# An eight-core transformer layer on Trainium2: V's second half, Wo's load, up's weights, the late AV copies and the x1 transposes at other places

## The reference, cut to what matters

```python
# x: (8, 2048, 1024) f32; 16 heads of 64
q, k, v = x @ Wq.T + bq, x @ Wk.T + bk, x @ Wv.T + bv
scores = einsum('bqhd,bkhd->bhqk', q, k) * hd ** -0.5
scores = scores * exp(-alpha * abs(i - j))        # i, j: positions
att = softmax(scores) @ v                         # per head, then joined
x1 = layernorm(x + att @ Wo.T + bo)
gate, up = fp4_linear(x1, w_gate), fp4_linear(x1, w_up)     # 2816 wide
h = silu(gate) * up
out = layernorm(x1 + fp4_linear(h, w_down))
# fp4_linear quantises both operands in blocks of 16 along the contracted
# dimension to an E2M1 grid and multiplies the dequantised values
```

## Time and profile before

| | us |
|---|---|
| median of 3 runs | 1275.07 |
| lowest, highest | 1273.63, 1281.92 |
| the profiled execution: its time | 1273.74 |
| its span on the slowest core (core 2) | 1272.2 |
| spans of all cores | 1261.7 to 1272.2 |

### The profile page before, as it was taken

The page is one execution under the profiler, slowest core; times in us unless marked ns, Lnnn a source line. Parts: engine busy times, 40 slices in busy tenths (PEclk is TensorE's granted clock), DMA queues, the critical chain, the costliest instruction groups (busy, mean ns, idle before and its releaser), DMA issues.

```text
span 1272.2 us, 18941 instructions; the slowest of 8 cores (1261.7 to 1272.2 us)
## 1 busy us (share of the span) xinstructions
PE 1156.1 (91%) x5787; PEld 460.6 (36%) x5856; DVE 1032.2 (81%) x1328; ACT 706.2 (56%) x841; POOL 257.7 (20%) x444
## 2 busy tenths in 40 slices
PE   3969999999999889999988886999999999999994
PEld 1413333333333223332322232444444444444442
DVE  4659999998988999997995476689888888888873
ACT  2148989888889899998998122222222222222221
POOL 1002222222222222322322343000101111111001
PEclk9979999999999999998998898999999999999998
DMA  9455646465454556675559369933333333334231
GB/s 247 166 116 137 146 118 156 117 127 126 110 140 120 140 129 152 148 167 151 159 157 261 86 205 299 315 113 110 81 91 82 81 93 81 81 92 126 67 68 61
DMA packets 180118, 172.58 MB, mean 136 GB/s; under 512 B 141938, under 2 KB 141938, under 8 KB 178484
## 3 DMA queue, kind: packets, MB, share of 16 engines
q1 hardware_dynamic: 165716, 138.72, 40.0%
q0 software_dynamic: 14304, 32.65, 10.9%
HBM read 111.30 MB, written 34.34 MB: 114 GB/s over the span
## 4 chain that ended last, share of the span: by engine, by line
PE 49%; DVE 16%; DMA 11%; issue 10%; ACT 9%; SPq 2%; POOL 2%; DVEq 0%; POOLq 0%; ACTq 0%
PE ps L1072 15%; PE ps L622 10%; PE ps L1154 8%; PE ps L501 7%; PE ps L456 6%; ACT PT L593 5%; PE ps L451 3%; DMA ring<-x_scr 3%; DVE fr L240 2%; DMA wos<-wo 2%; DMA vst<-wv 2%; DVE attnT L671 1%; ACT PT L601 1%; DVE qr L240 1%; SPq L1025 1%
## 5 line engine op out<-in xcount | busy, mean ns | idle before, releaser
L593 ACT ACTIVATE PT<-ps,tab 128x1024 bf16<-128x1024 f32 x384 | 414.1, 1130 | 72.5 <-PE ps L501 72.0
L622 PE MATMUL ps<-PT,V 128*128 128x512 bf16 (+1 forms) x1234 | 290.9, 341 | 10.1 <-issue 3.9
L501 PE MATMUL ps<-Q,KT 64*128 64x512 bf16 (+1 forms) x1280 | 205.8, 343 | 28.1 <-DVE SD L552 12.8
L1072 PE MATMUL ps<-wgT,x1qT 128*128 128x512 bf16 (+1 forms) x768 | 169.4, 364 | 10.8 <-DMA x1qT<-x1q 9.3
L1072 PE MATMUL ps<-wuT,x1qT 128*128 128x512 bf16 (+1 forms) x768 | 168.2, 362 | 0.5 <-DVE fs L242 0.3
L456 PE MATMUL ps<-xTs,wqk 128*128 128x512 bf16 x499 | 140.2, 386 | 26.3 <-ACT xTs L276 17.4
L1154 PE MATMUL ps<-wdT,hqT 128*128 128x512 bf16 x704 | 154.6, 379 | 0.3 <-DMA hqT<-hq 0.3
L622 PEld LDWEIGHTS ps<-PT,V 128*128 128x128 bf16 x1280 | 92.3, 98 | 156.1 <-issue 135.3
L501 PEld LDWEIGHTS ps<-Q,KT 64*128 64x128 bf16 x1280 | 54.4, 93 | 213.0 <-issue 211.9
L895 ACT ACTIVATE junk<-ring 128x1024 bf16<-128x1024 f32 x15 | 15.9, 1057 | 197.7 <-DVE ring L1165 197.7
L1082 ACT ACTIVATE sg<-ps 128x512 f32<-128x512 f32 (+1 forms) x96 | 50.7, 553 | 114.5 <-PE ps L1072 108.6
(11 more groups left out here) (96 smaller groups left out, 1292.9 us busy)
## 6 DMA issues: line engine op xcount, KB each, us to landing
ring<-x_scr SPq DMA_DIRECT2D x32, 512.0 KB, 5.2
wst<-wg SPq DMA_DIRECT2D x22, 512.0 KB, 4.3
wst<-wu SPq DMA_DIRECT2D x22, 512.0 KB, 4.1
wst<-wd SPq DMA_DIRECT2D x16, 704.0 KB, 5.1
xst<-xT SPq DMA_DIRECT2D x8, 1024.0 KB, 27.5
recD<-rec_scr POOLq DMA_DIRECT2D x64, 128.0 KB, 3.8
out<-ring POOLq DMA_DIRECT2D x15, 512.0 KB, 5.4
wg_scr<-wtr SPq DMA_DIRECT2D x22, 256.0 KB, 2.1
```

Of the source, the lines that this page charges most:

```text
L501: return op(TE, a, lambda e: e.matmul(out=out, lhsT=KT[hp % 2][r0:r0 + 64, kt * 128:(kt + 1) * 128], rhs=QR[u % 3][n][r0:r0 + 64, q0:q1], ...
L593: f = op(AC, k0, lambda e: e.activation(out=PT[ri], in_=src, func=AF.Exp, scale=scl), need)
L622: tok = op(TE, ka, lambda e, h=h, k=k, c0=c0, q0=q0, w=w: e.matmul(out=ps_ab[h][:, q0:q0 + w], lhsT=VV[g][:, k, hp % 4, 8 * h:8 * h + 128] ...
L1072: tk = fop(TE, t0, lambda e, i=i, wT=wT, pst=pst: e.matmul(out=pst[g][:, 0:F], lhsT=x1qT[tt % 2][:, i, :], rhs=wT[:, n0:n0 + nn, i, :], st ...
```

## The change

- The 16 jobs of V's second half go to units 1 to 15, two of them to unit 3; before they went to units 0 to 15, one each. Unit 0 then has K(1,0) and K(1,1).
- From unit 24 on the first half of the AV product, too, is copied by VectorE, just before the second half.
- Wo is loaded in four DMAs of two of its eight parts each, with the keys `at(30, 1 + 6 i)` = 481, 487, 493 and 499 on POOL. Job 0 waits for the last.
- The x1 transposes have the key X0 + 50 + 10 tt (576 and 586 for tiles 0 and 1) where it was X0 + 58 + tt.
- The six loads of up's weights are started by ACT, with the same keys.

```diff
@@ jobs
         for u in range(NU - 2):
-            if u < 16:
-                jobs[u] = vj[:1] + jobs[u]
-                vj = vj[1:]
+            if 0 < u < 16:
+                n = 2 if u == 3 else 1
+                jobs[u] = vj[:n] + jobs[u]
+                vj = vj[n:]
@@ put_norm
-            ev = [op(AC, max(ka + 0.1, at(u, 15) + 2.15), lambda e: e.activation(
-                out=AVs[s][0], in_=ps_ab[0], func=AF.Identity), [av, norm.get(u - 2)]),
-                dv(ka + 0.1, 0.68, lambda e: e.tensor_copy(
+            if u < 24:
+                ev0 = op(AC, max(ka + 0.1, at(u, 15) + 2.15), lambda e: e.activation(
+                    out=AVs[s][0], in_=ps_ab[0], func=AF.Identity), [av, norm.get(u - 2)])
+            else:
+                ev0 = dv(ka + 0.09, 0.68, lambda e: e.tensor_copy(
+                    out=AVs[s][0], in_=ps_ab[0]), [av, norm.get(u - 2)])
+            ev = [ev0, dv(ka + 0.1, 0.68, lambda e: e.tensor_copy(
                     out=AVs[s][1], in_=ps_ab[1]), [av, norm.get(u - 2)])]
@@ Wo
-        t_wo = op(PO, at(30, 9), lambda e: e.dma_start(
-            out=wo, in_=wo_h.rearrange("p (c d) -> p c d", d=D)), [t_pj], sem=d_wo, k=16)
+        wo_r = wo_h.rearrange("p (c d) -> p c d", d=D)
+        for i in range(4):
+            t_wo = op(PO, at(30, 1 + 6 * i), lambda e, i=i: e.dma_start(
+                out=wo[:, 2 * i:2 * i + 2], in_=wo_r[:, 2 * i:2 * i + 2]),
+                [t_pj], sem=d_wo, k=16)
@@ start_x1, done_
-                b_ = max([t_ + 0.05, X0 + 58.0 + tt] + ([xt_last[tt - 2].at + 0.01] if tt >= 2 else []))
+                b_ = max([t_ + 0.05, X0 + 50.0 + 10.0 * tt] + ([xt_last[tt - 2].at + 0.01] if tt >= 2 else []))
@@ the loop over job_w
-                    t_wu[c] = fop(SP, pe[0] - 2.0 + 0.1 * c, lambda e, n0=n0, nn=nn: e.dma_start(
+                    t_wu[c] = fop(AC, pe[0] - 2.0 + 0.1 * c, lambda e, n0=n0, nn=nn: e.dma_start(
                         out=flat(wuT[:, n0:n0 + nn]), in_=wus_r[:, n0:n0 + nn, :]),
                         gate, sem=d_wu[c], k=16)
```

## The result

The changed kernel takes 1286.22 us (median of 13 runs; 1273.86 for the kernel before, taken beside it). The ratio is 1.0072 [1.0046, 1.0097]: slower by 9 us where I had forecast 18 us faster, and above the upper end of my range (1267). That is within 1% of before, a result to which the prediction gave a chance of 0.17.

What follows compares the result with a forecast made beforehand. TensorE, busy 91% of the span, was taken as the bound, with gains only where it stands still. Terms -11 + 0 - 7.4 - 1 + 1 = -18.4 us took 1273.74 to 1255.3, 1256.7 as median, stated as 1256, range 1246 to 1267.

Steps and rivals of the forecast that it cites:

- V, taken as -11: Attention: unit 0 loses its stop and one job (-13.5 us), unit 3 pays +2.1, VectorE +0.5; range -13 to -8.
- +0.5, between 0 and +3: Unit 0: us lost to VectorE's third quantisation chunk, whose load lands about 76.9 when VectorE would be there at about 74.
- The AV copies, taken as 0: Units 24 to 31: TensorE holds the pace to 27, unit 28's gain is given back; 0 us (-2 to +3).
- rival D: Attention: the planner's search passes its limit, takes the next slack and crowds VectorE in every unit; 1286 us, chance 0.04.
- Wo, taken as +0.8: The w stage: job 0 starts 4.2 us later, a 3.45 us wait goes, the stage ends 0.8 us later (-2.5 to +4).
- +1 to +7: Before the w stage: range in us around job 0's 4.2 later start; the first piece may also delay unit 29's chain.
- The transposes and ACT's queue, taken as -8.2 in the wait before gate: Before gate: transpose 0 takes 10 us with only x's last load ahead; gate starts at 785.5, 7.4 us earlier than 792.90.
- Rival A: Before gate: transposes gain nothing from their own queue, transpose 0 takes 15.3 us, gate only 2.2 us earlier; 1263, chance 0.13.
- What starts it sets the end, one for one: FFN: one unbroken stretch of TensorE from 793 us on, so an earlier start ends it earlier by as much.
- The clock and up's weights, taken as -1 and +1: Gate's start: less idle raises the granted clock, -1 us (0 to -2); up's last loads may come late, +1 (0 to +4).
- B: Attention gives back unit 0's gain: Wo's first piece and fuller VectorE delay units 29 and 30; +6, 1262 us, chance 0.12.
- C: All falls well: faster Wo pieces (w stage -2.5), transpose 0 in time, full clock, unit 0 better; 1248 us, chance 0.11.

Runs made afterwards that it cites:

- v_delay: Kernel before with V's second half from unit 1 on and its casting load started later, by the scores of step 3 of unit 0: 1271.08 us, ratio 0.9964.
- av_noplan: Kernel before with the late AV copies on VectorE, recorded so that the planner of the quantisation doesn't see them: 1276.81 us, ratio 1.0016.
- wo_only: Kernel before with only Wo's load changed, to four pieces at the four keys: 1279.84 us, ratio 1.0034.
- no_act: Changed kernel with up's weights started by SP again instead of ACT: 1278.81 us, ratio to the kernel before 1.0011.
- keys_only: Kernel before with only the new keys of the x1 transposes: 1275.15 us, ratio 1.0000.
- t_first: Kernel before with the transposes' new keys, x1 tile 2 read back earlier, and up's last five loads behind transpose 1 on SP: 1269.88 us, ratio 0.9951.
- av_only: Kernel before with only the late AV copies moved to VectorE: 1281.91 us, ratio 1.0030.
- act_only: Kernel before with only the loads of up's weights moved to ACT: 1280.99 us, ratio 1.0048.

## Why the prediction was wrong

**V, taken as -11, is -6 to -7.** The mechanism held: the stop is gone, unit 3 pays. The term that was mis-sized is "+0.5, between 0 and +3" for VectorE's third chunk. I gave it its late arrival (about 3 us), and believed most of it hidden, though I had written that "the diagonal blocks queue behind it". They do: on core 7 VectorE waits 3.33 us for the chunk and TensorE 3.03 us for SD behind it, and without that wait (v_delay) unit 23 ends 2.0 us earlier. A second term the sum didn't have at all: TensorE waits 1.67 us for SD at 70.5 us, ahead of the third chunk, on every core; the stop had hidden it. A third is the row that I took: core 2's stop of 11.84 us is the longest of the eight cores, whose median is 10.9.

**The AV copies, taken as 0, cost 3 us at the median core.** The engines' balance was read rightly for units 24 to 27. The step that failed is that the planner was checked for its last place only (492.7 against the 493.6 of rival D), not for what its new order does to single units: units 28 and 30 grow by 1.5 and 3.1 us, far over the 0.6 a unit of the upper bound, and the w stage, of which I hadn't thought here, by 2.1. That is the planner's half of the cost, by av_noplan; the other half is the copies, which I took as hidden, and how they cost it stays open.

**Wo, taken as +0.8, costs some 3 us.** Its order and the absorption in the w stage were right, with 4.7 us given back for the forecast 3.4. What failed is the size of the delay. The forecast started job 0 4.2 us later than before; in wo_only it starts 10.2 us later at the median (706.7 to 716.9), some 3 us of it in attention and 7 behind it. I had allowed "+1 to +7", with the first piece's effect on unit 29 in brackets. On core 2 that effect is 4.7 us of the 5.5 that were missing, at the median 2.7 of 6. And that four pieces land later than one even at the old place (22.3 for 18.8 us) isn't in my account at all.

**The transposes and ACT's queue, taken as -8.2 in the wait before gate, are +6.3: the wrong sign, and the largest miss.** The step that failed is the choice of the nearest row: "a transpose with just such a load of 0.5 MB ahead in its own queue and 1 MB running in POOL's: 11.1 us". That row holds one load in another queue; here three start there while the transpose flies, 0.8 to 5.4 us after it on core 2, and one started 3.3 us before it is still under way. I counted what was ahead in the queue and not what was in flight beside it. Before, up's later loads stood behind the transpose on SP, and the next one started 8.7 us after it (core 2): the order was its protection, and the change took it away. Of the Trainium skill ("DMA: Bandwidth & Descriptors", "Issuing engines are not separate DMA queues") the trace bears out the sentence that I set against the gain: what ACT starts shares the engines, and only the issue is saved. Rival A took it at its word and still gave 15.3 us, since it, too, asked whether the queue ahead matters. The same page of the Trainium skill ("Queues, rings and completion order") says that each engine takes turns between the queues it has work for. I read this as help for the transpose, and it speaks against it: a queue beside the transpose's own takes turns from it. The trace agrees, as the 12.3 us of no_act become 21.6 in the changed kernel.

**"What starts it sets the end, one for one" holds only if all that the FFN is fed with moves along.** keys_only is the counterexample: 5.0 us in, none out. In the changed kernel it did not come to that, since gate started late.

**The clock and up's weights, taken as -1 and +1, had no chance to show.** Gate's first 16 matmuls take 5.4 us before and 5.8 after (medians over the cores), at a granted clock of 0.56 to 0.73 and 0.55 to 0.72, as the wait is still there. The term itself was sound: in t_first, where TensorE hardly waits, they take 3.6 us at 1.00. And of up's weights, sent off early, TensorE never has to wait in the changed kernel.

**The rivals.** B's mechanism (recD late, VectorE in order behind it) is there: such waits are 11.1 us a core, 6.5 before. C and D didn't come. The 1286 us of D are the measured time only by accident: the planner stops at the same slack of 0.6 as before. No rival ended slower than before for the reason that did it.

## What to carry to other kernels

A transfer on which the first matmuls wait is protected when the large loads stand behind it in its own queue; before a load is given to another engine's queue, ask what it will then fly beside. When a stop is removed, follow the next arrival on every engine with its full lateness, and when a start is moved, check that what feeds the stage moves with it. An automatic planner is to be checked for its order in each unit, not for its last place alone.

## What the runs showed of the hardware that I had not expected

On single cores the DMA engines crawl for 10 to 20 us: busy by their share and moving little. In core 7 of after it is the window 680 to 690 us (1.10 and 68 GB/s), with a transpose of VectorE's chunk that landed 24.6 us after its start, a piece of Wo that took 21.8, and den's 2 KB 19.7; in core 6 of v_delay it is 70 to 85 us, with a transpose (22.1 us) and V's load (25.4). No other core in the profiled executions of these kernels has such a window (10 us with a share over 0.9 and under 80 GB/s, from 30 to 1240 us). Both times a transpose and a casting load of POOL were in flight together; other cores have the same pair without harm, and no run tried that pair by itself, so the cause is open. It may matter because the slowest core is the metric: a core is over 8 us above the median of its execution in 4 of 88 core spans of after, 4 of 80 of av_only and of no_act and 3 of 80 of v_delay, against 7 of 840 of before in all sets, and 0 to 2 in each of the other kernels. Of all these only two were profiled: core 7 of after, which crawls, and core 0 of act_only, 8.9 us above its median, which doesn't. The crawling core of v_delay is 7.5 us above its median.
